# State scan of a gated delta layer: identity matmuls added to TensorE's list of every step

## The reference, cut to what matters

```
def step(state, inp):
    q_t, k_t, v_t, a_t, b_t = inp
    state = a_t[..., None, None] * state
    stored = jnp.einsum('bhij,bhj->bhi', state, k_t)
    delta = b_t[..., None] * (v_t - stored)
    state = state + jnp.einsum('bhi,bhj->bhij', delta, k_t)
    o_t = jnp.einsum('bhij,bhj->bhi', state, q_t)
    return (state, o_t)
```

## Time and profile before

| | us |
|---|---|
| median of 3 runs (lowest, highest) | 4119.48 (4111.95, 4126.69) |
| the profiled execution's own time | 4122.16 |
| its span, first to last instruction | 4120.4 |
| state scan, first read to last write | 938.1 to 1435.1 |
| TensorE busy over the span | 2660.1 (65%) |
| VectorE busy over the span | 2279.7 (55%) |
| ScalarE busy over the span | 1246.8 (30%) |
| mean granted TensorE clock | 0.737 |

### The profile page before, as it was taken

How to read it: one execution, slowest core, us unless ns; L and a number is a source line. 1 busy time by engine, 2 the same in 40 slices (tenths; PEclk the granted TensorE clock), 3 DMA queues, 4 the chain that set the end, 5 groups by cost and what they waited for, 6 DMA issues and landing times. The chain is left out here.

```text
span 4120.4 us, 91537 instructions
## 1 busy us (share of the span) xinstructions
PE 2660.1 (65%) x34356; PEld 1875.9 (46%) x34356; DVE 2279.7 (55%) x5471; ACT 1246.8 (30%) x3021; POOL 539.6 (13%) x613
## 2 busy tenths in 40 slices
PE   5986876238888746554666468777882019999800
PEld 2554544235555523332333346555562019999700
DVE  2485656725666568886611457667766014444466
ACT  3664553225666501111300034334431002222200
POOL 0221211000000001110000001001010650000065
PEclk8997877555555578887776589888895559999955
DMA  2536465663333284402097632121211422222255
GB/s 99 188 126 241 159 249 181 239 215 97 104 100 102 89 208 124 123 20 84 21 399 299 240 145 68 54 67 54 68 50 48 164 90 71 70 70 71 83 167 178
DMA packets 413008, 538.32 MB, mean 131 GB/s; under 512 B 178932, under 2 KB 341712, under 8 KB 403408
## 3 DMA queue, kind: packets, MB, share of 16 engines
q1 hardware_dynamic: 361840, 381.38, 28.8%
q0 software_dynamic: 39616, 127.22, 8.5%
q10 hardware_dynamic: 11296, 26.22, 1.6%
HBM read 329.68 MB, written 216.15 MB: 132 GB/s over the span
## 5 line engine op out<-in xcount | busy, mean ns | idle before, releaser
L1021 ACT ACTIVATE ss_write_ps<-ss_state,ss_gammas 128x64 f32<-128x64 f32 x1024 | 263.3, 302 | 195.6 <-DVE ss_state L1069 195.6
L443 PE MATMUL dc_rows_ps<-dc_weights,dc_hT 128*128 128x512 f32 x512 | 291.3, 698 | 8.5 <-issue 4.8
L1193 PE MATMUL do_late_ps<-do_scratch,do_ident 128*128 128x512 f32 (+1 forms) x416 | 197.2, 632 | 109.7 <-DVE do_scratch L1228 109.7
L2546 PE MATMUL se_up_ps<-se_xT,se_w 128*128 128x128 f32 x2176 | 267.5, 277 | 0.1
L500 PE MATMUL dc_solve_ps<-dc_sides,dc_blocks 32*32 32x32 f32 x8192 | 123.4, 226 | 215.0 <-ACT dc_blocks L594 99.0
L2554 PE MATMUL se_y_ps<-se_w,se_aT 128*128 128x256 f32 x1088 | 257.2, 380 | 0.0
L2546 PEld LDWEIGHTS se_up_ps<-se_xT,se_w 128*128 128x128 f32 x2176 | 255.9, 193 | 0.5 <-DVE se_w L2611 0.5
L2611 DVE COPY se_w<-mx_weights 128x2048 f32 x136 | 166.7, 1227 | 100.4 <-issue 100.4
L2682 POOL DMA_INDIRECT cb_y<-scratch_ys,cb_to x128 | 137.6, 1075 | 593.0 <-DVE cb_to L2697 554.6
L500 PEld LDWEIGHTS dc_solve_ps<-dc_sides,dc_blocks 32*32 32x32 f32 x8192 | 110.8, 138 | 228.5 <-ACT dc_blocks L594 119.0
L2554 PEld LDWEIGHTS se_y_ps<-se_w,se_aT 128*128 128x128 f32 x1088 | 196.6, 191 | 20.9
(11 more groups left out here) (346 smaller groups left out, 5650.1 us busy)
## 6 DMA issues: line engine op xcount, KB each, us to landing
ex_w<-in_w_all SPq DMA_DIRECT2D x64, 1024.0 KB, 21.2
scratch_rows<-dc_rows POOLq DMA_DIRECT2D x64, 512.0 KB, 4.2
scratch_vw<-dc_out POOLq DMA_DIRECT2D x64, 512.0 KB, 4.5
dc_c_rows<-scratch_rows SPq DMA_DIRECT2D x64, 384.0 KB, 4.6
scratch_xs<-wa_zeros ACTq DMA_DIRECT2D x34, 512.0 KB, 13.5
se_xs<-scratch_xs SPq DMA_DIRECT2D x136, 128.0 KB, 2.1
scratch_ys<-se_y SPq DMA_DIRECT2D x136, 128.0 KB, 1.7
ss_wq_rows<-scratch_vw SPq DMA_DIRECT2D x128, 128.0 KB, 2.2
```

Of the source, the lines that this page charges most:

```text
L443: mm = pe.matmul(to, hT[n % 2][:, k, :], weights[:, k, columns], start=(k == 0), stop=(k == HALVES - 1), skip_group_check=True)
L1021: ins = act.activation(write_ps[b][:, k, 0:WIDTH], state[b][:, k, :], ACT.Copy, scale=gammas[i][:, b, k, c:c + 1])
L1193: mm = pe.matmul(late_ps[:, to:to + (2 - skip) * DIM], ident[:, :], scratch[lag % 2][:, (t + skip - lag) * DIM:(t + 2 - lag) * DIM], start ...
L2546: mm = pe.matmul(up_ps[i % 2][:, c * P:(c + 1) * P], w[i % (2 * AHEAD)][:, k * DFF + c * P:k * DFF + (c + 1) * P], xT[i % 2][:, k, :], sta ...
```

## The change

A function `fill(c)` issues one matmul of the 128 x 128 identity with itself into columns 128 to 255 of half 0 of one of the two transposition banks. It is called in every step between the reads and the writes, behind the transposition's half 0 where there is one, and once more after the writes in every step that has no transposition. In the turning steps it takes the bank into which the step transposes, in the others bank 0. In step c = 5 (`TURN_AT + SETS`) TensorE first waits until ScalarE and VectorE have copied one of the earlier blocks out. Nothing is removed, and no other engine's list changes.

```diff
+                def fill(c):
+
+                    bank = (c - TURN_AT) % 2 if TURN_AT <= c < TURN_AT + SETS else 0
+                    pe.matmul(turn_ps[bank][:, 0, P:2 * P], ident[:, :], ident[:, :], start=True, stop=True, skip_group_check=True)
+
                 def tile_pair(ii, more):
                     for i in both:
                         tile = ii * 2 + i
...
                             if turning:
                                 turn(tile + 1, 1 - i, ii + i, c - TURN_AT, 0)
+                            if c == TURN_AT + SETS and (more or i == 0):
+                                pe.wait_ge(wq_low, at((tile + 1) * SETS + SETS - 1))
+                                pe.wait_ge(wq_high, at((tile + 1) * SETS + SETS - 1))
+                            fill(c)
                             for b in range(BATCH):
                                 pe.wait_ge(decay_ready[b], at(tile * N + c + 1))
                                 pe.wait_ge(u_ready[b], at(tile * N + c + 1))
...
                             if turning:
                                 turn(tile + 1, 1 - i, ii + i, c - TURN_AT, 1)
+                            else:
+                                fill(c)
```

## The result

The changed kernel takes 4282.44 us (median of 3 runs, 4282.13 to 4289.26), the kernel before 4119.48: a ratio of 1.0411, with a 95% interval of 1.0393 to 1.0429. It is 163 us slower. The forecast was 4058 us; what happened is the first rival, whose price was 4295, so the time lies inside the range (4030 to 4305) and on the other side of no change.

The account below looks back on a forecast made before the run. Latencies bound the scan's steps without transposition, TensorE's list the turning steps. With the clock risen, 68 us less, minus 6 for a late rise, gives 62 off 4122.2: 4060, or 4058 us as median; range 4030 to 4305.

Parts of the forecast that it names:

- Rival 1: Scan: the clock stays at 0.50 and fills are pure load on TensorE's ordered list, 176 us more, 4295 us; chance 0.38.
- Does the clock rise?: Scan: whether fills lift TensorE's clock from 0.50 to 1.00; called close to even, leaning to a rise, chance 0.53.
- Price of a fill at 0.50: TensorE's list in scan steps: one fill costs 0.73 us alone, some 0.43 us behind a transposition.
- The steps at 0.50: Scan steps with fills: 2.69 us without transposition, 2.47 us turning, together 176 us more.
- Rival 2: Scan: the clock stays at 0.50 because transpositions in turning steps don't count as busy; 4295 us, chance 0.03.
- The steps at 1.00: Scan steps with fills, clock up: 1.64 us without transposition, about 1.62 turning, together 68 us less.
- Not the bound: SyncE's queue: its wait of 4.1 us per tile shrinks to about 2, so it would not limit the scan.
- The added wait in step c = 5: TensorE's wait for copies made a step or more before: costs nothing; if late, under 10 us over 31 times.
- rival 3: Scan: the clock rises late or falls again; half the tiles at each clock gives +57 us, 4176 us; chance 0.06.

Follow-up runs that it names:

- wide fills: The changed kernel with each fill moving 256 columns instead of 128: 4192.32 us, ratio 1.0178 to the kernel before.
- fills of the reads' shape: The changed kernel with each fill at 32 stationary columns instead of 128, same rows and moving columns: 4098.07 us, ratio 0.9973 to the kernel before.
- burst and fills: The changed kernel with 20 more identity matmuls back to back just before the first step: 4283.69 us, ratio 1.040 to the kernel before.
- the best version: The kernel before plus fills of 32 stationary and 128 moving columns, in turning steps ahead of the first transposition: 4063.72 us, ratio 0.9877.
- store first: The kernel before plus 32-stationary-column fills (192 moving columns ahead of transpositions, 128 elsewhere), SyncE issuing stores ahead of loads: 4066.96 us, ratio 0.9889.

## Why the prediction was wrong

*Does the clock rise?* is the step that failed. It counted how long all 128 rows take in data in a step at 0.50 (1.5 to 1.7 of 2.47 to 2.69 us), held that against the token choice's 16 transpositions without gaps, and leaned to a rise. The clock stayed at 0.50 in all 663.6 us. Two things were weighed wrongly. First, the count gave the writes, on 16 rows, a full 0.43 us or half of it; only with more rows streamed in the same kind of step (wide fills) or the same rows in a step 0.61 us shorter (fills of the reads' shape) did the clock rise. That the writes count for little fits this, but no run changed them alone, so it isn't shown. Second, the sentence "after each change of shape nothing streams for 0.1 to 0.15 us" stood there as a remark against the rise, and the one change that a run let measure took 0.14 us; what it didn't see is that in a step without transposition the 128-column fills double such changes, from two to four, and bring two longer weight loads, and that both can be had back. The price of 0.73 us for 0.43 us of streaming was the warning: at that ratio a fill lengthens the step nearly as fast as it fills it.

*Price of a fill at 0.50*: right. Forecast 0.73 us alone and 0.43 behind a transposition; measured 0.72 to 0.73, and 2.48 - 2.04 = 0.44. The 0.10 us in it for the weight load came from the shortest of eight in the earlier trace rows (285 ns); their median, 333, would have made the price 0.78, so the exact hit is in part luck. *The steps at 0.50*: 2.69 and 2.47 forecast, 2.67 and 2.48 measured. The sum of 176 us came out 166.6: 5.15 us more per tile (20.57 against 15.42), where four steps of either kind sum to 5.4. Half of the difference is step c = 6, which the sum took as 1.76 us like its neighbours and which took 1.91 (reads at 1200.95 and 1202.86 in the kernel before), with VectorE's last copy ahead of its subtraction; that idle time took up a part of the fills. Rival 1 was right in mechanism and within 13 us of the time. It had a chance of 0.38, and should have had the larger one: the only row on the disputed question from the scan itself, turning steps with two full-width records at 0.50, spoke for it.

*Rival 2* (transpositions hold the clock down) is contradicted: in burst and fills, with wide fills and in the best version, turning steps run at 1.00, in the latter for 388 us up to the end of the scan. The falls in turning steps go with the waits there, since all 14 that were counted stand beside one, and with the fill in that time, at the same size, they are gone. That the wait alone drops the clock is not shown: 45 of them passed without a fall in one run, and 66 with wide fills.

*The steps at 1.00*: the order of size was right, the turning step wasn't. Forecast 1.64 and 1.62 us; with burst and fills the steps without transposition took 1.6 to 1.9 and the turning steps 1.6, 1.7 and then 1.96 twice, a tile 14.2 to 14.5. The forecast had VectorE's copy late for its own subtraction, but not for the next transposition, which waits for that bank. The best version's tile, 13.5 us, is near the forecast 13.2 to 13.4 all the same, but with another fill in another place, so that is no hit of the forecast. One small slip in the sum: eight records with half of 0.022 us less between them save 0.08 us and not 0.06 to 0.07, so the circle would be 1.41 us and not 1.44; nothing else hangs on it. *Not the bound*, of SyncE's queue, held in the steady part, where store first gave tiles of the same length at 1.00 (the queue's wait was 78.3 us in the best version, 65 forecast), and failed in the third tile, where the queue is still behind: there it cost 2.49 us in burst and fills, and the clock fell within that wait.

*The added wait in step c = 5*: nothing at 0.50, as forecast; no row of TensorE in the changed kernel shows it. At 1.00 it was not nothing: 0.23 us in each tile (998.94 and 1112.82 above), 7 us if it were so 31 times, which is within the 10 us that the forecast gave for a late copy. *A clock that rises late or falls again* (rival 3, 0.06) did not happen in the changed kernel, but in most of its variants, so it was too small a case for a state that changed so often from one tile to another.

## What to carry to other kernels

Filler work for the clock has a price and an effect that have to be worked out at the lower clock, since that is where it must lift it: here 0.73 us of an ordered list for 0.43 us of streaming lifted nothing, and the same rows in the shape of the neighbouring matmuls did. Put the filler where the engine already waits, ahead of the instruction that waits and not behind it; with an ordered list the place decides its cost, and here the clock held better too. And if the forecast rests on a state that the stretch in question never shows, the case in which nothing changes there deserves the larger chance.

## What was not expected of the hardware

TensorE 99% busy by its records ran at 0.50 for 663.6 us, so busy time alone doesn't lift the clock. And the same list can run at either clock: with full-width fills it ran at 1.00 for 54.6 us behind a burst before it fell, and at 0.50 it never rose in 663.6 us. The clock fell within a single wait of TensorE of 2.49 us; one of 1.30 us was followed by a fall 2.3 us after its end. Steps with wide fills ran eight tiles at 0.50 before the clock rose without a visible reason, and the fills of the reads' shape lost it six times in 195 us and then not at all in 226, with the same list. What decides the moment is open.
